# A transformer layer with ternary feed-forward: the first feed-forward tile moved into the last attention tile, and the tasks of a step redistributed

## The reference, cut to what matters

```
x = x + attn(layernorm(x))      # x: 16 sequences x 2048 tokens x 1024
x = x + ffn(layernorm(x))

attn: q, k, v = split(x @ w_qkv)          # 16 heads of 64
      scores = q k^T / 8, allowed where i-128 < j <= i
      out = softmax(scores) v;  return out @ w_out
ffn:  h = bitlinear(x, W1, b1); h = gelu(h) (exact); return bitlinear(h, W2, b2)
bitlinear(x, W, b):
      s  = mean|W|;         Wq = clip(round(W / s), -1, 1) * s       # ternary
      xs = max|x| of a row; xq = round(x * 127 / xs) * xs / 127
      return xq Wq^T + b                                            # hidden size 4096
```

## Time and profile before

| | us |
|---|---|
| median of 3 runs | 1684.28 (1682.67 to 1684.78) |
| the profiled execution: its time | 1682.09 |
| its span on the slowest core | 1680.6 |
| PE busy | 1533.8 (91%) |
| DVE busy | 1095.2 (65%) |
| ACT busy | 862.4 (51%) |
| POOL busy | 226.4 (13%) |
| DMA, share of 16 engines on SP's queue | 40.4% |

### The profile page before, as it was taken

How to read it: one execution, slowest core, us unless ns; L and a number is a source line. 1 busy time by engine, 2 the same in 40 slices (tenths; PEclk the granted TensorE clock), 3 DMA queues, 4 the chain that set the end, 5 groups by cost and what they waited for, 6 DMA issues and landing times.

```text
span 1680.6 us, 34852 instructions; the slowest of 8 cores (1674.7 to 1680.6 us)
## 1 busy us (share of the span) xinstructions
PE 1533.8 (91%) x12228; PEld 864.5 (51%) x12228; DVE 1095.2 (65%) x2683; ACT 862.4 (51%) x1941; POOL 226.4 (13%) x136
## 2 busy tenths in 40 slices
PE   1699999999999888844999999999999999999998
PEld 1477776666666655621444444444444444444443
DVE  2366688887888888854666666656565656666652
ACT  2699988887888656631333333333333333342431
POOL 0010000000000000005012121212121212121200
PEclk9899999999999999966999999999999999999998
DMA  8745554544444444342324342424343333434331
GB/s 263 257 150 166 165 160 156 152 152 153 156 158 152 139 133 129 113 125 81 82 63 107 63 110 66 108 67 103 73 98 78 93 85 86 94 76 93 77 82 51
DMA packets 211324, 198.09 MB, mean 118 GB/s; under 512 B 173904, under 2 KB 174032, under 8 KB 211024
## 3 DMA queue, kind: packets, MB, share of 16 engines
q1 hardware_dynamic: 206544, 179.08, 40.4%
q0 software_dynamic: 4608, 16.78, 2.7%
HBM read 120.32 MB, written 33.55 MB: 92 GB/s over the span
## 4 chain that ended last, share of the span: by engine, by line
PE 76%; DVE 11%; issue 5%; DMA 4%; ACT 2%; SPq 1%; DVEq 0%; POOL 0%; ACTq 0%; POOLq 0%
PE f L199 30%; PE av L199 27%; PE sc L199 15%; DVE msc L458 3%; PE tA L204 2%; PE tB L204 2%; DVE tern L220 2%; DVE lnc L333 2%; DVE PT L248 1%; DVE W2q L661 1%; DMA wst<-wqkv 1%; DMA wst<-wout 1%; DVE xr L235 1%; SPq L185 1%; DMA b1b<-b 1%
## 5 line engine op out<-in xcount | busy, mean ns | idle before, releaser
L199 PE MATMUL av<-W2q,hqT 128*128 128x512 fp8e4 x2048 | 450.0, 381 | 3.5 <-DMA hqT<-hq 3.5
L215 ACT ACTIVATE hbuf<-hb 128x512 f32<-128x512 f32 x256 | 161.2, 630 | 471.6 <-DVE hb L232 471.5
L199 PEld LDWEIGHTS av<-W2q,hqT 128*128 128x128 bf16 x2048 | 201.3, 98 | 247.1 <-issue 7.5
L199 PE MATMUL f<-xlnT,wqkv_sb 128*128 128x128 bf16 x4096 | 255.9, 222 | 50.5 <-ACT vh L215 20.8
L215 ACT ACTIVATE probs<-msc,cells 128x256 bf16<-128x256 f32 (+1 forms) x512 | 250.7, 493 | 57.2 <-DVE cells L458 56.3
L199 PEld LDWEIGHTS f<-xlnT,wqkv_sb 128*128 128x128 bf16 x4096 | 238.4, 99 | 60.6 <-issue 60.5
L199 PE MATMUL sc<-W1q,xqT 128*128 128x512 fp8e4 x1024 | 236.5, 385 | 35.4 <-DMA xqT<-xq 31.5
L199 PE MATMUL f<-W1q,xqT 128*128 128x512 fp8e4 x1024 | 231.5, 379 | 0.0
L458 DVE CUSTOM_DVE_ANT_0 msc<-sc,masks 128x256 f32<-128x256 f32 (+1 forms) x512 | 182.2, 412 | 47.5 <-PE sc L199 31.5
L215 ACT ACTIVATE hq<-hbuf,konst,fhc 128x1024 f16<-128x1024 f32 x128 | 148.3, 1229 | 87.9 <-DVE fhc L220 87.9
L199 PEld LDWEIGHTS sc<-W1q,xqT 128*128 128x128 bf16 x1024 | 101.0, 99 | 161.0 <-issue 43.5
(11 more groups left out here) (81 smaller groups left out, 1474.8 us busy)
## 6 DMA issues: line engine op xcount, KB each, us to landing
stg<-w1t SPq DMA_DIRECT2D x64, 512.0 KB, 4.1
stg<-w2t SPq DMA_DIRECT2D x64, 512.0 KB, 4.0
xr<-xc SPq DMA_DIRECT2D x32, 512.0 KB, 4.8
x1sp<-xr POOLq DMA_DIRECT2D x32, 512.0 KB, 4.0
x1r<-x1sp SPq DMA_DIRECT2D x32, 512.0 KB, 4.9
y<-yb SPq DMA_DIRECT2D x32, 512.0 KB, 3.3
wst<-wqkv SPq DMA_DIRECT2D x24, 512.0 KB, 15.0
wst<-wout SPq DMA_DIRECT2D x8, 512.0 KB, 19.2
```

What stands on the lines that cost most here:

```text
L199: return op("pe", lambda e: e.matmul(out=out, lhsT=lhsT, rhs=rhs, start=start, stop=stop), waits, sig)
L215: return op("act", lambda e: e.activation(out=out, in_=in_, func=func, **kw), waits)
```

## The change

- Layer-normed rows and attention output are transposed by DMAs in SP's queue (`x_tr`, `at_tr`) in place of TensorE and ACT. The second identity matrix is gone.
- `ln1` is split: the statistics (`ln1_stats`) stay at c = 3, `ln1_rstd` (ACT) and `ln1_nmr` (DVE) are at the end of c = 0 of the next tile, followed by GpSimd's `xln_` and the transpose. `ln2_sum`, `ln2_sq` and `spill` move to the same place, one tile later (tile t-2). The load of x moves to c = 1.
- Tasks: six staging buffers up to task 95, two after. Two tasks in each third step up to step 39 and in five steps of 40 to 79, one in the others; the last is in step 110. Even a1 tasks are a DVE reduction, the others stay with ACT. The comparison of a quantization goes to GpSimd (`task_pool`, at the head of the step, output 8 bits wide); DVE's half stands after the first filler in steps c = 1 and at the end of the step else. The copy of transposed probabilities goes to ACT in steps c = 3 with a q2 task.
- The feed-forward's buffers are laid over others, so that it can begin early: tile 0 is reloaded and quantized in tile 30, the biases are loaded (in five pieces) once the last V matmuls have read the weights, and units 0 to 5 of tile 0's first layer are the fillers of tile 31 at c = 0, 1 and 3. Units 6 and 7 and the output projection of tile 31 (into the bank `av`) follow, then the loop as before, without its former first pass.

```diff
+        def x_tr(t):
+            tk["xlnT", t] = dma_tr(xlnT[t % 2], xln, d_xlnT[t % 2],
+                                   [tok("xln", t), tok("V", t - 2, 1)])
...
-            tk["PT", j] = tfree[b] = vcopy(o, i, [tok("T", j), tok("AV", j - 2)])
+            w = [tok("T", j), tok("AV", j - 2)]
+            tk["PT", j] = tfree[b] = (act(o, i, AF.Copy, w) if on_act
+                                      else vcopy(o, i, w))
...
+        def at_tr(t):
+            tk["attnT", t] = dma_tr(attnT, attn, d_at,
+                                    [tok("N", t, 0), tok("N", t, 1),
+                                     tok("O", t - 1, 1)])
...
+        def slot(n):
+            return n % 6 if n < 96 else n % 2
...
         def task_load(n):
...
+            k = slot(n)
+            task_ld[n] = dma("sp", stg[k], task_src(kind, i), d_stg[k],
+                             [tok("task", prior[n]), tok("w", 3, "a"),
+                              tok("w", 3, "v")])
...
+        def task_pool(n):
+            kind, i = tasks[n]
+            g = 0 if kind[1] == "1" else 1
+            tk["tern", n] = ts("pool", tern[n % 2], stg[slot(n)],
+                               wsc[:, 5 * g + 2:5 * g + 3], None, ALU.is_lt,
+                               waits=[task_ld[n], tok("thr", g),
+                                      tok("ternq", n % 2)])
...
+        def load_bias(i):
+            if i < 4:
+                tk["b1", i] = dma("sp", b1b[:, i * D:(i + 1) * D],
+                                  b1_d[i * D:(i + 1) * D].partition_broadcast(
+                                      128), d_bias[i], [tok("V", nt - 1, 1)])
...
+        def ubank(t, u):
+            return (2, 3, 2, 3, 2, 3, 0, 1)[u] if t == 0 else u % 4
...
+        for j in range(1, nstep):
+            k = 1
+            if j < 40 and j % 3 == 0:
+                k = 2
+            elif 40 <= j < 80 and j % 8 == 5:
+                k = 2
...
+            while to_load and (prior[to_load[0]] is None or
+                               tok("task", prior[to_load[0]]) is not None):
+                task_load(to_load.pop(0))
+            for n in mine:
+                if n == 32:
+                    scale_pe(0)
+                if n == 96:
+                    scale_pe(1)
+                if tasks[n][0][0] == "q":
+                    task_pool(n)
+            if c == 1 and 2 <= t and t + 3 < nt:
+                load_x(t + 3)
             if nxt:
                 s_pe(j + 1)
                 ttr(j + 1)
             if prev_ev is not None:
                 prev_ev()
...
             if f1 is not None:
                 f1()
-                e1()
...
+                e1() if c != 2 and not late else None
+            for n in mine:
+                if tasks[n][0][0] == "a":
+                    task_run(n)
+            if c == 1:
+                for n in mine:
+                    if tasks[n][0][0] == "q":
+                        task_run(n)
             if nxt:
                 ex(j + 1, 2)
                 ex(j + 1, 3)
             if j >= 1:
                 av_pe(j - 1)
+            if c == 0 and t >= 1:
+                norm(t - 1, 1)
+                at_tr(t - 1)
+            if c == 2 and f1 is not None:
+                e1()
+            if c == 2:
+                norm(t, 0)
             t_pe(j)
+            pt_ev(j, on_act=(c == 3 and any(n >= 96 for n in mine)))
...
+            if c != 1:
+                for n in mine:
+                    if tasks[n][0][0] == "q":
+                        task_run(n)
+            if c == 0:
+                if t >= 2:
+                    ln2_sum(t - 2)
+                    ln2_sq(t - 2)
+                if t + 2 < nt:
+                    ln1_rstd(t + 2)
+                    ln1_nmr(t + 2)
+                    xln_(t + 2)
+                    x_tr(t + 2)
+                if t >= 2:
+                    spill(t - 2)
             if c == 3 and t + 3 < nt:
+                ln1_stats(t + 3)
+
+            if t == nt - 2:
...
+                if c == 3:
+                    xt(0)
+                    for i in range(5):
+                        load_bias(i)
...
         lt = nt - 1
         av_pe(nstep - 1)
+        for u in (4, 5):
+            pre_gelu(0, u)
         norm(lt, 1)
+        at_tr(lt)
+        for u in (6, 7):
+            w1_pe(0, u)
+            pre_gelu(0, u)
+        xt(1)
+        hmax(0, 0)
+        hmax(0, 1)
+        for u in range(4, 8):
+            gelu(0, u)
         for h in range(2):
+            o_pe(lt, h, av[:, h * 512:(h + 1) * 512], tok("N", lt, 1))
+            resid(lt, h, av[:, h * 512:(h + 1) * 512])
+        hmax(0, 2)
+        hmax(0, 3)
+        fh(0)
+        for r in range(4):
+            rnd(0, r)
+            unoff(0, r)
+        for t in (lt - 1, lt):
+            ln2_sum(t)
+            ln2_sq(t)
+            spill(t)
...
+        front_pool(2)
+        add_bias(2)
+        front_dve(2)
```

406 lines of the change are left out of this document (182 added, 224 removed).

## The result

The changed kernel takes 1696.95 us (median of four runs), the kernel before 1683.5 us on the same chip: ratio 1.0075, 95% interval [1.0055, 1.0095]. In some executions, of whatever kernel, cores of one die or both run at a lower granted clock and take some per cent longer (here 1781.04 us beside 1694.78, 1695.89 and 1698.02), and such executions are left out of every ratio. The forecast was 1655 us with a range of 1615 to 1685. So the change makes the kernel 0.75% slower, where it was forecast to be 1.7% faster, and the time lies outside the range. The profiled execution took 1694.78 us, its slowest core 7 has a span of 1693.2 us, and the cores lie between 1678.7 and 1693.2 (before: 1674.7 to 1680.6). In the mean of the eight cores the span rose by 7.9 us; the wider spread of the cores adds 4.7.

What follows compares the result with a forecast made beforehand. Attention was taken as bound by TensorE at first and DVE at the end, feed-forward by TensorE. From 1682.1 us, start +3, loop +14 and changeover -46 gave 1653; the runs' median lies 2.2 higher: 1655, range 1615 to 1685.

Steps and rivals of the forecast that it cites:

- What bounds the kernel: Whole kernel: attention bound by TensorE at first, DVE at the end; feed-forward's TensorE full; changeover's busy 32.91 of 71 us.
- A new wait on DVE: End of a tile's first step: DVE waits for ScalarE before the small product, 1.9 us a tile.
- The comparison goes to GpSimd: Quantizations: comparison takes 2.85 us on GpSimd; DVE idles 3.3 us in 18 tiles with one in the second step.
- (a): Rival on quantizations: GpSimd's comparison is cheap, 1.2 us, total 30 us less at 1625; chance 0.22.
- (b): Rival on quantizations: GpSimd becomes the bound, slower than before, 1712 us at a 6 us comparison; chance 0.13.
- The loop, kind by kind: Attention tiles: +13 us in tiles 6 to 19, +14 in 20 to 27, -13 in 28 to 30; loop +14.
- Six slots, more loads. Nothing: Task loads: land in 4.1 us, so six slots, and two in the last phase, cover them; no cost.
- Removed transposes: Attention tiles: TensorE loses 0.92 us of work a tile, 19.5 to 18.6 us.
- rival (c): Attention tiles: DMA transposes land late, each microsecond late in 30 tiles costing 30 us; chance 0.10.
- The start: Before the loop: -4 for the second identity, +4 for transposes among weight pieces, +3 for task loads; +3 us.
- The changeover: Head of tile 31 to first second-layer matmul: 53.2 us instead of 99.3, so -46 us.
- rival (d): Changeover gives less, -33 us instead of -46, total 1668 us; chance 0.07.

Runs made afterwards that it cites:

- a3: Changed kernel with the logarithm, exponential and small product of tile t+2 put ahead of mean and square of tile t-2: 1666.31 us.
- a2: Changed kernel with the quantization's comparison back on DVE, right ahead of DVE's second half: 1684.53 us.
- c1: a3 with six staging slots kept to task 107 instead of 95: 1654.17 us.
- b1: Kernel before with only the comparison moved to GpSimd (8 bits, two buffers, at the head of the step): 1679.77 us.
- c3: Changed kernel with the edits of a3, c1, a4 and a5 together: 1655.63 us.
- c5: c3 with no quantization in a second step from task 108 on, the last in step 118 instead of 110: 1634.26 us.
- b2: Kernel before with only both transposes (layer-normed rows, attention output) made DMAs: ratio 1.0188, from two runs.
- a7: Changed kernel with both transposes on TensorE and ScalarE again: 1682.02 us.
- a4: Changed kernel with two task loads before the loop instead of six, not waiting for the weight casts: 1701.14 us.
- a5: Changed kernel with tile 1's quantization later and tile 2's GpSimd work earlier in tile 31: 1698.37 us.
- a1: Changed kernel with DVE's half of a second-step quantization at the end of the step, as in the others: 1696.68 us.
- c7: c5 with both transposes on TensorE and ScalarE again, and the edit of a1: 1621.63 us.

## Why the prediction was wrong, step by step

- **What bounds the kernel**: right. Feed-forward did not change, and the changeover gave the largest gain.
- **"A new wait on DVE"**: the chain and its place were right, and the wait was 65.7/32 = 2.05 us in the mean against 1.9. Its price was wrong. It was added as DVE idle time of its own; but it stands at the head of the second-step chain, through normalization, spill issue and comparison to TensorE's products. The other order (a3) takes 44 us of this wait away (65.7 to 21.7) and gives 30.6 us: 2.4 us in each of the ten tiles 6 to 19 with a second-step quantization and 0.4 in the four others. By the sum's slope the square alone, 1.15 us in 28 tiles, would be 32 us; that this is near 30.6 is luck, since neither the amount nor the tiles are the same. And the wait was set down as a cost of the change as such, though the order of two groups of instructions in one block decides it, and that order was not questioned.
- **"The comparison goes to GpSimd"**: 2.85 us taken, 2.847 measured over 64 instances. The second-step wait of 3.3 us was 3.63 in the chain above, and the tiles 9, 11, 12 and 15 are 3.1 us shorter without it (a2). Rivals (a) and (b) fall. The prediction also says that its 1.248 us row agrees with an estimate of 1.5 us at best; the row is below that, so it does not, and 2.847 us is far above.
- **"The loop, kind by kind"** is the first failed step: 21.9 and 24.1 us a tile were DVE's busy time plus DVE's waits. In tiles 6 to 19 the miss is in the ten tiles with a second-step quantization, 23.3 us instead of 21.9; the four others take 19.9 (forecast 19.7). Tile 12 has 15.07 us of DVE work (the sum had 15.5 for 2.25 quantizations, 15.2 for its two), so the work was right; its idle time is 8.3 us and not 6.4. The two named waits are 6.1 of it (forecast 5.2); the "rest" of 1.2, taken over from the old order on the ground that the new waits overlap it, is 2.2. More than half of it, 1.28 us, comes from TensorE: idle 2.64 us behind DVE's copy, and then 4.2 us at a granted clock of 0.59. A wait of DVE in the second step becomes one of TensorE, is paid in part again by the clock, and returns to DVE as a wait for scores. Tiles 9 and 11 separate that part: the same waits, with and without a fall of the clock, 23.38 and 22.07 us. The 14 tiles came to 27.7 us more instead of 13.
- **"Six slots, more loads. Nothing"** is the second failed step, and the plainest. It compared a load's 4.1 us with one step, and left out who frees the buffer: from the head of the step to DVE's half at its end, then the load, now 4.7 to 5.8 us, then the comparison. c1 (-12 us from twelve tasks more on six slots), b1 (+5 us in tiles 28 to 30 from the comparison's place alone) and c3's tiles on six and on two slots (21.7 and 24.7 us) show it from three sides. These tiles missed the forecast of 192.8 us by 10.7; c1 takes 11.3 off them, a number near to it, though on top of a3. c5's further 24.3 are not the trip alone: it takes quantizations out of these tiles, and with them second-step waits.
- **"Removed transposes" and rival (c)**: the 0.92 us of TensorE a tile came true where nothing else bounds (18.58 in tile 28, 18.7 forecast). Rival (c), given 0.10, has the direction right: the DMAs cost 30 us in the old order (b2) and 15 in the new one (a7), of which the start is 6.4. Its mechanism, TensorE waiting for a late `attnT`, is shown for 22 us of b2 and hardly at all in the changed kernel (one wait, of 1.7 us). The forecast priced the DMAs as a term of the start alone; what they do to the landing time of the loads (4.1 to 5.8 us) had no term.
- **"The start"**: +3 forecast, +2.7 measured, which is luck: a4 shows the task loads' share near nothing (forecast +3), a7 that the transposes' is 6.4 (forecast +4). With TensorE's transposes the head of tile 1 is at 79.2 against 82.9 before, about the -4 of the estimate for the second identity.
- **"The changeover"**: 59.1 us instead of 53.2. On core 7, 60.65: +2.5 in tile 31, -0.5 to the scale, +3.4 from the scale to the next tile's first matmul, +2.0 for matmuls at a low clock. The +3.4 is the kept 9.5 us, "in the same order now": in the new order GpSimd's `add_bias` runs at the same time, and the unoffsets take 6.52 us with their waits, against 3.83 in a5. The stall for the bias loads came in another form than priced: `attnT` of tile 30 was not waited for, the first bias load was. Why a5, which removes the slow unoffsets, shows only 1.2 us in this stage in the mean is not settled. The gain of 38.9 us lies between the forecast's 46 and rival (d)'s 33.
- **Tiles 28 to 30**: 59.7 instead of 56, all in tile 30 (22.78 us): the quantization of feed-forward's tile 0 was moved there, and its DVE work was not in the sum.
- **The cores' spread** was not in the forecast at all: 4.7 of the 13 us by which the time rose. It arises ahead of tile 6; tile 1 takes 18.6 to 25.2 us on the different cores, and on core 7 TensorE waits 4.5 us there for the transposed rows. a4, which aimed at this wait, did not mend it.

## What to carry to other kernels

Add waits along the path on which they stand, not per engine: two waits on one path are not priced apart (here either edit alone gave the same 3.1 us a tile), and an exchange of order that freed a small product from a 1.15 us square ahead of it was worth 31 us. Two buffers cover a load only if the whole round trip (producer's landing, both consumers, the queue's next issue) fits into the two steps; price it whenever one of its links moves to a slower engine. A sum that comes out right does not show that its terms are: look at the tiles in which the time moved (a2, a3, the start). And an edit that gives nothing (a1) can be worth its price once the bound beside it is gone (c7), so it is tried again after each larger one.

## What the runs showed of the hardware

- GpSimd's comparison to 8-bit output, f32 input of 128x1024, takes as long as its subtraction to f32: 2.847 us median, 2.836 to 3.680, against 2.846 us in the earlier trace rows.
- A DVE scaling from f16 to bf16 of 128x1024 takes 0.43 us alone (a5) and up to 2.56 us while GpSimd adds two f32 tensors of 128x1024 (changed kernel).
- Behind a TensorE wait of 2.6 us the granted clock was 0.59 for 4.2 us, and the tile 1.3 us longer than one with the same wait and no fall; six of the ten waits over 2.4 us in tiles 6 to 19 were followed by a fall. In a3 no wait in these tiles was over 1.7 us, and core 1 shows no fall in them.
- A DMA transpose of 128x1024 lands in 3.1 to 4.3 us median in the changed kernel, and the W1 loads of 512 KB take 5.8 us beside them, 4.7 without (a7); in the old order it was 4.4 with them (b2) and 4.1 without.
